# A fused convolution, attention and expert kernel: the product of probabilities and values on pairs of 64-column tiles

## What is computed

```python
q = jnp.einsum('bsd,ed->bse', x, Wq)
k = jnp.einsum('bsd,ed->bse', x, Wk)
v = jnp.einsum('bsd,ed->bse', x, Wv)
scores = jnp.einsum('bqd,bkd->bqk', q, k) / jnp.sqrt(jnp.float32(d))
scores = jnp.where(causal, scores, jnp.float32(-jnp.inf))
weights = jax.nn.softmax(scores.astype(jnp.float32), axis=-1)
out = jnp.einsum('bqk,bkd->bqd', weights, v)
```

## Time and profile before

| | |
|---|---|
| median of three runs | 479.53 us (476.7 to 480.04) |
| the profiled execution, time | 476.61 us |
| the profiled execution, span from first to last instruction | 474.8 us |
| PE busy | 386.0 us (81%) |
| PEld busy | 285.4 us (60%) |
| DVE busy | 388.7 us (82%) |
| ACT busy | 267.3 us (56%) |
| POOL busy | 240.6 us (51%) |
| mean granted TensorE clock (1 is 2.4 GHz) | 0.911 |
| the chain that ended last, by engine | DVE 49%, PE 37%, issue 7%, ACT 3%, POOL 2% |

### The profile page before, as it was taken

One profiled execution on the slowest core, in us unless ns is written; L12 is line 12 of the kernel. 1 busy time (PEld: TensorE's weight loads), 2 busy tenths in 40 slices (PEclk: granted clock), 3 DMA queues, 4 the chain that ended last, 5 costly groups with the idle time before them and its releaser, 6 DMA issues.

```text
span 474.8 us, 7502 instructions
## 1 busy us (share of the span) xinstructions
PE 386.0 (81%) x3006; PEld 285.4 (60%) x3006; DVE 388.7 (82%) x599; ACT 267.3 (56%) x342; POOL 240.6 (51%) x139
## 2 busy tenths in 40 slices
PE   1289789898995979799999797899978778763796
PEld 1278557565764656556777575577747435443485
DVE  3898789899989698979898979798997988875432
ACT  0114348667665767567866665777756748821500
POOL 5314535564758476945463759463648743142000
PEclk9999889899998899989999999999998979985555
DMA  4600000000000000000000000000005000000033
GB/s 116 147 2 1 0 0 1 2 1 2 1 1 0 1 1 1 1 2 0 1 1 1 0 1 1 1 2 1 1 0 91 1 1 0 1 1 1 0 89 89
DMA packets 15919, 6.75 MB, mean 14 GB/s; under 512 B 5967, under 2 KB 15757, under 8 KB 15885
## 3 DMA queue, kind: packets, MB, share of 16 engines
q1 hardware_dynamic: 13168, 5.62, 4.9%
q10 hardware_dynamic: 2717, 0.66, 0.7%
HBM read 4.16 MB, written 2.11 MB: 13 GB/s over the span
## 4 chain that ended last, share of the span: by engine, by line
DVE 49%; PE 37%; issue 7%; ACT 3%; POOL 2%; DMA 1%; POOLq 1%; SPq 0%; DVEq 0%
DVE negmax L683 15%; PE psB L809 10%; DVE M L690 6%; DVE Pp L376 5%; DVE M L689 3%; PE psA L980 3%; PE psA L799 3%; PE psB L939 3%; PE psB L951 2%; DVE x_all L599 2%; PE psA L944 2%; PE psB L917 2%; PE psA L809 2%; PE psA L894 2%; PE psB L879 2%
## 5 line engine op out<-in xcount | busy, mean ns | idle before, releaser
L683 DVE TENSOR_REDUCE negmax<-psA 128x1 f32<-128x1024 f32 (+7 forms) x128 | 89.6, 746 | 23.4 <-PE psA L905 23.4
L376 POOL TENSOR_TENSOR Pp<-e,Pp 128x1024 f16<-128x1024 f32 x45 | 95.9, 2143 | 14.8 <-ACT Pp L528 14.8
L527 ACT ACTIVATE e<-psB 128x1024 f32<-128x1024 f32 (+1 forms) x80 | 75.2, 940 | 32.6 <-PE psB L920 26.6
L528 ACT ACTIVATE Pp<-psB 128x1024 f16<-128x1024 f32 (+1 forms) x80 | 75.4, 942 | 0.0
L939 PE MATMUL psB<-Pp,zV 128*64 128x512 f16 (+3 forms) x384 | 65.6, 327 | 1.5 <-ACT Pp L528 1.5
L429 POOL TENSOR_TENSOR zrstd<-zrstd,power 128x8 f32<-128x8 f32 x16 | 26.3, 1643 | 69.5 <-DVE zrstd L665 69.5
L809 PE MATMUL psA<-y,DD 128*128 128x224 f16 (+1 forms) x480 | 56.6, 277 | 1.9 <-DVE y L657 1.9
L809 PE MATMUL psB<-xin,UU 128*128 128x224 f16 (+1 forms) x480 | 56.2, 276 | 1.2 <-ACT lg L539 1.2
L939 PEld LDWEIGHTS psB<-Pp,zV 128*64 128x64 f16 x384 | 39.1, 110 | 27.2 <-ACT Pp L528 1.7
L902 PE MATMUL psA<-zK,yQ 128*128 128x512 f16 (+1 forms) x192 | 47.4, 329 | 9.7 <-DVE negmax L683 8.2
L809 PEld LDWEIGHTS psB<-xin,UU 128*128 128x128 f16 x480 | 47.4, 99 | 9.6 <-ACT lg L539 1.9
(11 more groups left out here) (158 smaller groups left out, 722.8 us busy)
## 6 DMA issues: line engine op xcount, KB each, us to landing
x_all<-in_x_dram SPq DMA_DIRECT2D x4, 512.0 KB, 4.7
out_dram<-x_all SPq DMA_DIRECT2D x8, 256.0 KB, 2.3
y<-in_L_ffn_weight_dram SPq DMA_DIRECT2D x3, 256.0 KB, 4.0
Pp<-filter_tables ACTq DMA_DIRECT2D x4, 121.9 KB, 3.3
cst<-shape_constants SPq DMA_DIRECT2D x1, 326.5 KB, 4.2
xin<-in_L_ffn_weight_dram SPq DMA_DIRECT2D x1, 256.0 KB, 4.4
Pp<-filter_tables ACTq DMA_DIRECT2D x1, 120.0 KB, 3.3
gw_sb<-in_L_ffn_gate_w_dram SPq DMA_DIRECT2D x4, 2.0 KB, 2.9
```

Of the source, the lines that this page charges most:

```text
L376: return engine.tensor_tensor(Pp[:, n % 2, 1, o:o + N], e32[:, (NU * n + i) % 3, 0:N], Pp[:, n % 2, 0, o:o + N], ALU.subtract)
L527: nc.scalar.activation(e32[:, m % 3, 0:N], slot(e)[:, 0:N], ACT.Exp)
L528: nc.scalar.activation(Pp[:, n % 2, 0, UOFF[e[2]]:UOFF[e[2]] + N], slot(e)[:, 0:N], ACT.Exp).then_inc(b_drained, 1)
L683: ins = nc.vector.tensor_reduce(negmax[:, n % 2, m - 1:m], s[:, at:at + P * m], X, ALU.max, negate=True)
```

## The change

pv loops over key tiles, parts and two halves of the queries by parity, instead of over contiguous halves. In a tile of 128 queries the columns are stored as four rows of 32; `probs_j` takes rows 0 and 2 (odd = 0) or 1 and 3 (odd = 1), 64 columns of each tile. The even ones are written to partitions 0 to 63 of the output, the odd ones to partitions 64 to 127, both into the same 512 columns. The weights, 64 columns of zV, are loaded for each matmul into the half of the array whose output it is. "pv" joins ONE_BANK, ScalarE's copy becomes 128 partitions by 512 columns, and oT has one slot for each of four batches. proj reads both batches' slots in turn, with the partition half now meaning parity instead of batch, and att is stored in a contiguous order. The bounds of t in schedule() are wider, which adds no event: the list of events is the same.

```diff
-ONE_BANK = ("gn_mean", ..., "tok", "zK", "zV", "hidden")
+ONE_BANK = ("gn_mean", ..., "tok", "zK", "zV", "pv", "hidden")
...
-        oT = sb("oT", [P, 2, S])
+        oT = sb("oT", [P, GB, BANK])
...
-                    nc.scalar.activation(oT[64 * (n % 2):64 * (n % 2) + 64, n // 2 % 2, :], slot(e)[0:64, :],
-                                         ACT.Copy).then_inc(b_drained, 1)
+                    nc.scalar.activation(oT[:, n % GB, :], slot(e), ACT.Copy).then_inc(b_drained, 1)
...
-                    av = att[:, :].rearrange("p (b k c) -> p k b c", b=GB, k=KT)[:, :, 2 * e[2]:2 * e[2] + 2, :]
+                    av = att[:, 2 * BC * e[2]:2 * BC * (e[2] + 1)].rearrange("p (k d) -> p k d", k=KT).rearrange("p k (r c) -> p k r c", r=2)
...
-                        for i in range(2):
-                            last = R * (i + 1) - 1
-                            if j > last:
-                                continue
-                            q = max(P * j, BANK * i)
-                            N = BANK * (i + 1) - q
-                            o = PLACE[j] + q - P * j
-                            by_row = s[0:2 * C, BANK * i:BANK * i + BANK].rearrange("p (r i q) -> p i r q", r=R, i=R)[:, R - N // P:R]
-                            for part in range(2):
-                                ins = nc.tensor.matmul(by_row, zV[:, n % 3, j, :], Pp[:, n % 2, part, o:o + N],
-                                                       start=j == 0 and part == 0, stop=j == last and part == 1)
+                        o, N = PLACE[j], P * (KT - j)
+                        for part in range(2):
+                            probs_j = Pp[:, n % 2, part, o:o + N].rearrange("p (t r q) -> p t r q", r=2, q=2 * C)
+                            for odd in range(2):
+                                rows = s[2 * C * odd:2 * C * odd + 2 * C, :].rearrange("p (r t q) -> p t r q", r=2, t=KT)[:, j:KT]
+                                ins = nc.tensor.matmul(rows, zV[:, n % 3, j, :], probs_j[:, :, :, C * odd:C * odd + C],
+                                                       start=j == 0 and part == 0, stop=j == KT - 1 and part == 1, skip_group_check=True)
...
                     for k in range(KT):
-                        ins = nc.tensor.matmul(s[:, P * k:P * k + 2 * C + 2], oT[:, e[2], P * k:P * k + P], V2[:, :], start=True, stop=True)
+                        b, a, r = k // 4, k // 2 % 2, k % 2
+                        at = S // 4 * r + P * a
+                        ins = nc.tensor.matmul(s[:, P * k:P * k + 2 * C + 2], oT[:, 2 * e[2] + b, at:at + P], V2[:, :], start=True, stop=True)
```

More of the change, by code:

```diff
@@ L147, in schedule @@
     events = list(FIRST)
-    for t in range(-6, B + 4):
+    for t in range(-9, B + 6):
         for event in STEP:
@@ L162 @@
 BANKS = 4
-ONE_BANK = ("gn_mean", "gn_var", "dnT", "shift", "down", "wT", "pool", "experts", "turned", "tok", "zK", "zV", "hidden")
+ONE_BANK = ("gn_mean", "gn_var", "dnT", "shift", "down", "wT", "pool", "experts", "turned", "tok", "zK", "zV", "pv", "hidden")
 def place(units):
@@ L697, in _ @@
                     sv = s.rearrange("p (k d) -> p k d", k=KT)
-                    av = att[:, :].rearrange("p (b k c) -> p k b c", b=GB, k=KT)[:, :, 2 * e[2]:2 * e[2] + 2, :]
+                    av = att[:, 2 * BC * e[2]:2 * BC * (e[2] + 1)].rearrange("p (k d) -> p k d", k=KT).rearrange("p k (r c) -> p k r c", r=2)
                     link(nc.vector.reciprocal(rsum[:, e[2], :, :], sv[:, :, 2 * C:2 * C + 2]))
-                    nc.vector.tensor_tensor(av, sv[:, :, 0:2 * C].rearrange("p k (b c) -> p k b c", b=2),
+                    nc.vector.tensor_tensor(av, sv[:, :, 0:2 * C].rearrange("p k (r c) -> p k r c", r=2),
                                             rsum[:, e[2], :, :].unsqueeze(3).broadcast_to([P, KT, 2, C]), ALU.mult).then_inc(a_drained, 1)
```

## The result

The changed kernel took 490.01 us in the median of 3 runs (488.27 to 490.19) against 479.53 before: 1.0224 times as long, with a 95% interval of 1.0153 to 1.0295. So it is slower by 10.5 us. The prediction was 482.7 us with a range of 475 to 490; the direction it leaned to was right, the size was not, and the time is 0.01 us above the range.

What follows compares the result with a forecast made beforehand. VectorE and TensorE were taken to wait for each other once per batch, with pv in VectorE's stretch. Clock falls +4.0, banks +0.9 and tail -1.7 gave +3.2 us: 482.7 from the median 479.53, range 475 to 490.

Steps and rivals of the forecast that it cites:

- pv: Product with the values on TensorE: 32 paired matmuls take 2.2 us instead of 4.09, a saving of 1.9 per batch.
- Hidden in VectorE's stretch: pv lies where VectorE is busy without a break, so its saved time only becomes a longer TensorE stand before the shift.
- The wait of VectorE between the maxima: In VectorE's stretch of row maxima: the forecast is wrong if VectorE waits for TensorE there; no size given.
- The last batch, put at nothing: Writing of the last batch's M, ahead of the last shift: the forecast's sum had no term for it.
- The price of a gap: TensorE's gaps before the shift: 3.9 clock falls at 1.55 us, +6.0, less a third: +4.0 us.
- The banks: pv in one bank makes prob 3 wait for ScalarE's drain of prob 2 in five periods: +0.9 us in all.
- The tail: From 405 us on, where pv is on the chain: pv, copy and output end sooner, -1.7 us.
- The signs: Profile after: TensorE's waits for M from 25.4 to 35 us or more, VectorE's after up from 23.4 to about 28.
- Slower by the clock (C): Rival: clock falls in every grown gap at full price and ahead of down in three bank periods: +10.5, 490 us; chance 0.20.
- the pairs don't overlap (B): Rival: pv stays at 4.2 us and the bank waits cost unpaid: +2.5, 482 us; chance 0.12.
- the loads are exposed (D): Rival: pv's weight loads no longer hide under matmuls, pv +3.3 us: 498 us; chance 0.05.
- the clock holds (E): Rival: no falls in grown gaps, and shifts at 270.92 and 362.31 start at full clock: -4.8, 474.7 us; chance 0.17.

Runs made afterwards that it cites:

- e1: The changed kernel with pv given two banks again, as before the change, pairs and smaller copy kept: 484.45 us, 1.0121 of the kernel before.
- e9: The kernel before with the low half of the probabilities left out of pv, 12 matmuls instead of 24: 483.22 us, 1.0100 of the kernel before.
- e11: Pairs and two banks for pv, with GpSimd's low part of unit 2 of batch 14 held until the last M is written: 480.01 us, 1.0012 of before.
- e2: The changed kernel with pv's same 32 matmuls reordered, all even queries first, then all odd; one bank kept: 480.42 us, 1.0033 of the kernel before.

## Why the prediction was off

The step that failed most is a term put at nothing, for the last batch. By the prediction's own steps:

- **pv.** 2.2 us forecast, 2.15 to 2.43 measured; the loads of 110 ns stay hidden, with the same rows of the array in use by load and matmul. Right. The Trainium skill's rule that a load overlaps only another row group (TensorE: Matmul & The Clock Gate, Part 3, what overlaps), by which pv would take over 7 us (an estimate from the rows), is not borne out by this trace: 32 loads of 110 ns are 3.5 us alone. The copy takes 0.60 us, as forecast.
- **Hidden in VectorE's stretch.** Right: e1 and e9 save 2 us in each pv and are not faster for it. The wait of VectorE between the maxima, named as a sign of error, did not come.
- **The last batch, put at nothing.** This step failed, and it is the largest part of the miss. The sum has no term for the last M: I followed what a faster pv does to TensorE and VectorE, and not that ScalarE, and through it GpSimd, start earlier against VectorE's M. The last shift came 2.95 us late through M, and its stretch cost 2.75 more at the low clock: 5.7 us in the trace, and about 5 by e11. The trace of before held the warning: the write of M took 0.23 us in the last batch, with GpSimd's pair starting only 0.17 us behind it, and 2.08 in others.
- **The price of a gap.** +4.0 forecast. Over the same stretches the pair of traces has +6.3: 1.55 at 177, 3.3 and 0.9 at 321 and 347, 0.9 at 298 and 0.6 at 394, less 0.95 at 203.5 where a fall went away; those at 106.88 and 128.34, which the forecast counted at five in seven each, cost nothing. In this trace the step that fails is "of these I take off a third, since a fall that begins some way into the section costs less than the 1.55 of the worst case shown": the 1.55 was no worst case, as the low level lasted 6.8 us behind 321. But this rests on one execution of each kernel. By the medians, e11 leaves 0.6 us (-1.2 to 2.4) for these falls and the tail together; with the trace's -2.0 for the tail that is some 2.6 for the falls, an estimate. So that the clock falls in grown gaps was right, and whether +4.0 was too small or too large stays open.
- **The banks.** In four of the five periods named prob 3 waits for the drain of prob 2, and in the period shown, set back by the 1.20 us that the trace is late there, down starts 0.8 us from where I had it. "I take zero for this period and for the one of 362.31" failed: the shifts there came 1.96 and 2.85 us later. The fall ahead of down, which I had priced at 1.5 and then set off against a fast shift, cost 1.0 and 2.2; and the set-off, -1.55 in the one, was only -0.26 in the other. In the period at 225 +0.9 was forecast and 0.33 measured; at 247 zero was right. In the terms of the forecast +0.9 was +3.3.
- **The tail.** -1.7 forecast; behind the last shift's stretch it is -2.0. Right in itself.
- **The signs.** TensorE's waits for M rose to 29.7 us, not to the 35 forecast, as the bank waits took the gaps' place in three periods (without them, in e1, they are 37.7); VectorE's waits rose to 24.5, not 28.
- **The rivals.** Slower by the clock (C), at 490 us, is the one whose number came, and that is luck in part: its falls in every grown gap at full price and its three ahead of down were not all there, and the last M, which it did not have, took their place. That the pairs don't overlap (B) and that the loads are exposed (D) are refuted by the 2.15 us of pv; that the clock holds (E) is refuted by the trace.

In sum, for the pair of traces: the gaps +4.0 were +6.3, the banks +0.9 were +3.3, a term of +5.7 was missing, the tail was about right and 0.3 was there from the start: 13.6 where I had 3.2, of which the medians show 10.5. What stays open is why a gap of 1.83 or of 2.12 to 2.19 us is followed by a fall in one place and by none in another; no run here looks into it.

## What to carry over

Time saved on an engine in a stretch where it waits anyway comes back as a longer gap, and on TensorE a longer gap can lower the clock of the stretch behind it, the one that counts; but one pair of traces does not price such falls, as they come at other places in other runs. When an engine off the path gets faster, look for which instruction of a third engine now starts sooner, and beside what. Small writes on the path beside long GpSimd instructions are worth a look first: one wait on GpSimd gave 4% here, the faster product nothing.

## What the runs showed of the hardware

- **VectorE beside GpSimd.** M's TENSOR_TENSOR of 128x16 takes 0.23 us alone and 2.07 beside a GpSimd instruction of 2.1; its CAST 0.20 alone and 1.67 there; the CAST of y (128x1024) 0.68 and 2.60, its TENSOR_TENSOR 1.23 and 3.04. In the rows of the last M the VectorE instruction ends within 0.1 us of the end of GpSimd's: it is not slowed in proportion to its size, it waits the other out. The Trainium skill (SBUF — State Buffer, Who interferes with whom) says that the two engines share a port pair that one of them holds for a whole instruction; this trace agrees.
- **Column halves.** Two neighbouring matmuls on the two 64-column halves run side by side: 9,216 columns in 2.15 us, 4.3 per ns, against 2.3 when the same matmuls stand in an order without pairs (e2).
- **The clock.** A fall can cost twice 1.55 us: the stretch from 322.18 to 329.00 lay at 0.50 throughout. Gaps of 1.83, 2.12 and 2.19 us brought one in some places and none in others: in e1 0.52 behind 1.83 at 226.28 and 1.00 behind 1.83 at 322.41.
